# Expert feed-forward in units of 128 rows, four to a group, with the transposed rows copied by VectorE

## The chip, the cores and the metric

The kernel runs on one core of a Trainium2 chip. The metric is the device time of one launch in microseconds. All times below are microseconds of device time unless marked ns. The compute engines are PE (TensorE), DVE (VectorE), ACT (ScalarE) and POOL (GpSimd); SP (SyncE) issues most of the transfers.

## The reference

A batch of 16 sequences of 512 tokens, width 128, passes through four residual blocks: a linear attention, a mixture of experts, a second attention that keeps the 6 strongest rows of each head, and the same mixture again. Cut to the part that the change touches (T = 8192 tokens, E = 16 experts, K = 2 choices, D = H = 128):

```python
x = x + attn_a(layernorm(x))
x = x + ffn(layernorm(x))
x = x + attn_b(layernorm(x))
x = x + ffn(layernorm(x))

def ffn(xf):                                   # xf: [T, D]
    w, idx = top_k(softmax(xf @ router_w), K)  # two experts for each token
    # each expert takes at most `capacity` first choices and as many second
    # choices, in token order; dispatch lists the tokens of each expert
    xe = x_pad[dispatch]
    gate = einsum('ecd,edh->ech', xe, gate_w)
    up = einsum('ecd,edh->ech', xe, up_w)
    out = einsum('ech,ehd->ecd', silu(gate) * up, down_w) * wbuf
    return zeros.at[dispatch].add(out)         # sum of a token's two rows
```

## The kernel before

Each engine has its own program, written out by hand; the order on an engine is the order in the source, and engines meet only in semaphores. The phases are: attention A over 16 batches, the experts of its mixture, attention B, the experts of the second mixture, and a tail that adds the experts' rows into the tokens and stores them.

**Stages.** Each mixture is cut into two halves of 8 batches, so `experts` runs four times. The text calls these stages 0 to 3 (`seg` in the code). Stage 1 follows stage 0 at once, attention B lies between stages 1 and 2, and stage 3 follows stage 2 at once. The tokens of a half are scattered to DRAM (`dispA` or `dispB`) by POOL's indirect transfers, one area for each expert, and the area is read in *units* of `UR` rows that belong to one expert. A table made on chip lists for each unit its first row and its expert. Half a mixture has 48 units of 256 rows, taken in 24 groups of `GU` = 2 units, so that a group is always 512 rows.

**One group, engine by engine.** SP's `load(seg, g)` reads the unit's row numbers from the table into registers (one TENSOR_LOAD, then a check of each value: FUSED_REGOPS and SEQ_ASSERT) and issues one transfer for each unit into `apart` (named `xe`). There are `NX` = 4 such buffers; loads 0 to 3 of a stage are issued ahead, and load g waits for the transposes of group g-4. PE's `turn_x` (L1812) transposes four tiles of rows into one PSUM bank. ACT's `xT` (L846) copies them to `xeT`. PE's `gate_up` (L1823) multiplies with the gate and up weights; ACT's `silu` (L851) and DVE's `hidden` (L1293) form the hidden rows; PE's `down` (L1834) multiplies with the down weights; DVE's `y_copy` (L1301) empties the PSUM bank into `ye`; SP's `store` (L417) writes that to `ybufA` or `ybufB`. PE's order is `turn_x(g+1)`, `gate_up(g)`, `down(g-1)`, then a piece of other work that belongs to group g (`pieces(g)`: routing of the last batches, the end of attention B, the tables of the next stage).

**Weights.** Since the expert of a unit is known only at run time, its 384 weight columns are copied from `f_w` into a ring of group buffers `unit_w`, at an address from a register: by POOL for the first four groups of a stage (L587), by ACT for the others (L858), each copy waiting until the buffer's last `down` is done.

**SP's order in a stage.** For g = 0, 1, ...: `load(g+4)`, then `store(g-2)`, which waits for `y_copy(g-2)`. After its last load of an even stage SP waits until the next stage's table is made and its tokens are sent (`ready`, L400 to L405), then issues load 0 and load 1 of the next stage, the third last store, load 2, the second last store, load 3, and the last store. `y_copy(g)` waits until the store of group g-2 has landed, because there are two `ye` buffers.

**After stages 0 and 2** POOL waits until all stores of the stage have landed (`stored`) and gathers the two expert rows of each token with indirect transfers (`fetch`, L564), eight for a batch. A fetch needs the batch's slot numbers (`slg`), and for batch b these are written by DVE once it has added batch b-2 (`add_all`, which ends in `indices(b + 2)`). In stage 3 DVE adds `EARLY` batches beside the groups, three groups to a batch, beginning at group 5; the others follow behind the stage. `EARLY` is (groups - 4) // 3.

The constants from which the sizes follow:

```python
UT = 2                       # tiles of 128 rows in a unit
UR = UT * P
GU = 2                       # units in a group
NX = 4                       # buffers of rows and of weights
UNITS = -(-(HALFB * SEQ * K // UR + E - 1) // (GU * NX)) * GU * NX
GRP = UNITS // GU            # groups in a stage
```

## Time and profile before

| what | value |
|---|---|
| median of three runs | 1403.18 (1398.74 to 1406.71) |
| the profiled execution | 1396.88 |
| its span, from the first to the last instruction | 1395.1 |
| busy shares of the span | PE 89%, DVE 75%, POOL 60%, ACT 54% |
| chain that ended last | PE 70%, DVE 12%, POOL 7% |

| stretch | from | to | length |
|---|---|---|---|
| attention A, until the first transpose of stage 0 | 0 | 341.6 | 341.6 |
| stage 0 and stage 1 (48 groups) | 341.6 | 503.0 | 161.4 |
| attention B | 503.0 | 1130.1 | 627.1 |
| stage 2 (24 groups) | 1130.1 | 1219.8 | 89.7 |
| stage 3 (24 groups), beside POOL's gathering for the first half | 1219.8 | 1298.7 | 78.9 |
| the rest of the gathering, adding and storing | 1298.7 | 1395.1 | 96.4 |

The share of busy time is a mean over these stretches, and they have different limits. In the expert stages the place to look is the time of one group on each engine and on SP, which is not counted as busy at all; in the tail it is POOL's line of indirect transfers. In a row of the timeline the first number is the start, the second the length, then engine, line, operation, what it writes and reads, and how many were merged; the bracket at the end is the idle time before it and what ended it.

### The profile page before, as it was taken

Reading aid. Unit: us, or ns where it says so; the run is one execution under the profiler, and the core shown is the slowest. Engines: PE = TensorE matmul, PEld = TensorE weight load, DVE = VectorE, ACT = ScalarE, POOL = GpSimd, SP = SyncE. Lnnn points to the kernel's source line nnn. Section 1 sums busy time; section 2 is a strip of 40 time slices with the busy share of each in tenths; the row PEclk is TensorE's granted clock in tenths of the full one; section 3 lists DMA queues with packets and bytes.
Section 4 is the critical chain, followed back from the end, with each engine's and each line's share of the span. In section 5 each row is a group of like instructions: output and inputs, shape, how many; then the busy total and the mean of one; then the engine's idle time right before and its main releaser. Section 6 shows DMA issues by size and latency. Waiting matters only on the chain.

```text
span 1395.1 us, 28372 instructions
## 1 busy us (share of the span) xinstructions
PE 1239.1 (89%) x8534; PEld 787.4 (56%) x8534; DVE 1042.0 (75%) x4462; ACT 756.4 (54%) x1901; POOL 836.4 (60%) x1246
## 2 busy tenths in 40 slices
PE   3999998996999999999999999999999999999100
PEld 1566665565898965454545445545455469888100
DVE  2899999895674458898999989989998856565322
ACT  2444444442665767666676756656676546556000
POOL 3237776777525224356777767766874445367776
PEclk9999999997999998998999989999999899999655
DMA  6845602011556520000100001011000125466522
GB/s 174 259 154 192 197 30 87 28 44 60 171 163 210 166 65 16 14 11 24 32 25 29 32 24 32 29 62 48 29 28 14 44 79 162 150 218 205 150 75 75
DMA packets 119783, 125.80 MB, mean 90 GB/s; under 512 B 15568, under 2 KB 109904, under 8 KB 119632
## 3 DMA queue, kind: packets, MB, share of 16 engines
q1 hardware_dynamic: 103248, 90.42, 20.5%
q0 software_dynamic: 16384, 33.59, 7.9%
q8 instruction: 68, 1.11, 0.3%
q14 instruction: 83, 0.68, 0.2%
HBM read 50.15 MB, written 73.79 MB: 89 GB/s over the span
## 4 chain that ended last, share of the span: by engine, by line
PE 70%; DVE 12%; POOL 7%; issue 4%; DMA 2%; ACT 2%; SPq 0%; POOLq 0%; ACTq 0%; DVEq 0%
PE pair L1897 25%; PE pair L1823 8%; POOL vmyg L564 6%; PE pair L1685 5%; DVE pT L1401 5%; PE bank L1709 4%; PE pair L1834 4%; PE pair L1812 2%; PE bank L1630 2%; PE bank L1624 2%; PE pair L1674 2%; DVE xs L1318 2%; PE bank L1936 1%; PE bank L1916 1%; PE pair L1695 1%
## 5 line engine op out<-in xcount | busy, mean ns | idle before, releaser
L1897 PE MATMUL pair<-kT,apart 32*128 32x512 f32 x2048 | 460.2, 672 | 3.5 <-DVE smax L1401 2.0
L1401 DVE CUSTOM_DVE_ANT_0 pT<-pair,pT 128x256 f32<-128x256 f32 x1024 | 384.2, 416 | 76.1 <-ACT pT L925 70.4
L925 ACT ACTIVATE pT<-pair 128x256 f32<-128x256 f32 x1024 | 327.0, 397 | 196.8 <-PE pair L1897 193.3
L1897 PEld LDWEIGHTS pair<-kT,apart 32*128 32x128 f32 x2048 | 192.8, 192 | 128.1 <-DVE smax L1401 78.7
L564 POOL DMA_INDIRECT vmyg<-ybufA,slg x128 | 123.7, 966 | 110.6 <-DVE smax L1401 67.9
L1823 PE MATMUL pair<-xeT,unit_w 128*128 128x256 f32 x768 | 184.6, 384 | 0.0
L564 POOL DMA_INDIRECT vmyg<-ybufB,slg x128 | 122.8, 959 | 71.3 <-DVE smax L1401 33.6
L509 POOL DMA_INDIRECT dispB<-xnf,sli x128 | 129.3, 1010 | 57.0 <-issue 35.2
L509 POOL DMA_INDIRECT dispA<-xnf,sli x128 | 130.0, 1016 | 50.9 <-issue 30.2
L1128 DVE TENSOR_TENSOR pT<-pair,causal 128x1024 f32<-128x1024 f32 x128 | 151.2, 1213 | 12.1 <-PE pair L1685 11.2
L1293 DVE TENSOR_TENSOR hid<-sg,pair 128x512 f32<-128x512 f32 x96 | 65.7, 685 | 123.3 <-ACT sg L851 123.1
L1823 PEld LDWEIGHTS pair<-xeT,unit_w 128*128 128x128 f32 x768 | 140.5, 193 | 15.5
L1318 DVE SCALAR_TENSOR_TENSOR xs<-vmyg,wts,xs 128x128 f32<-128x128 f32 x248 | 81.1, 379 | 75.4 <-DMA vmyg<-ybufB,slg 55.1
L1834 PE MATMUL pair<-unit_w,hid 128*128 128x128 f32 x768 | 102.1, 276 | 8.6 <-DVE ye L1301 8.4
L1834 PEld LDWEIGHTS pair<-unit_w,hid 128*128 128x128 f32 x768 | 99.9, 192 | 16.2 <-DVE hid L1293 10.6
L858 ACT ACTIVATE unit_w<-f_w 128x384 f32 x160 | 74.9, 515 | 50.1 <-PE pair L1834 47.8
L851 ACT ACTIVATE sg<-pair 128x512 f32<-128x512 f32 x96 | 57.3, 597 | 55.7 <-PE pair L1823 55.3
L1401 DVE DVE_READ_ACCUMULATOR2_ANT smax<- 128x1 f32 x1024 | 82.5, 81 | 0.0
L1685 PE MATMUL pair<-apart,kT 32*128 32x512 f32 x512 | 77.5, 647 | 1.8 <-DVE pT L1128 1.8
L1709 PE MATMUL bank<-pT,vmyg 128*32 128x128 f32 x2048 | 70.9, 280 | 0.0
L1301 DVE COPY ye<-pair 128x512 f32<-128x512 f32 x96 | 65.6, 683 | 6.7 <-DMA ybufA<-ye 4.0
L551 POOL TENSOR_SCALAR lnv<-mv 128x4 f32<-128x4 f32 (+1 forms) x51 | 11.9, 234 | 97.1 <-DVE mv L1024 89.0
(231 smaller groups left out, 1947.6 us busy)
## 6 DMA issues: line engine op xcount, KB each, us to landing
dispB<-zeros SPq DMA_DIRECT2D x16, 1408.0 KB
apart<-dispA SPq DMA_DIRECT2D x96, 128.0 KB
ybufA<-ye SPq DMA_DIRECT2D x48, 256.0 KB
apart<-dispB SPq DMA_DIRECT2D x96, 128.0 KB
ybufB<-ye SPq DMA_DIRECT2D x48, 256.0 KB
dispA<-zeros SPq DMA_DIRECT2D x33, 128.0 KB
xs<-in_x SPq DMA_DIRECT2D x16, 256.0 KB, 3.1
out<-xs SPq DMA_DIRECT2D x15, 256.0 KB, 2.6
```

The lines of the kernel that those rows point to most:

```text
L509: pool.indirect_dma_start(out=area, out_offset=bass.IndirectOffsetOnAxis(ap=sli[h][:, K * j + k:K * j + k + 1], axis=0), in_=xnf[g % NF][: ...
L564: pool.indirect_dma_start(out=yg[h][:, j, :], out_offset=None, in_=ybuf[second(g)], in_offset=bass.IndirectOffsetOnAxis(ap=slg[h][:, j:j + ...
L858: last = act.activation(unit_w[g % NX][:, u, :], f_w[:, bass.ds(ex[u], 1), :].rearrange("p a n -> p (a n)"), ACT.Copy)
L925: act.activation(rel[n % RING][:, q, :], pair[n % RING][:, q, HALF:SEQ], ACT.Relu).then_inc(s["relu_done"], 1)
L1128: dve.tensor_tensor(pTd[n % NG][:, :, :], pair[1 + n % 2][:, :, :].rearrange("p q (j t) -> p (q j) t", j=GH), causal[:, :].unsqueeze(1).to ...
L1318: last = dve.scalar_tensor_tensor(out=xb, in0=yg[h][:, K * j + k, :], scalar=wts[:, bass.ds((b * TB + j) * K + k, 1)], in1=xb, op0=ALU.mul ...
L1401: dve.tensor_tensor_reduce(out=rel[n % RING][:, q, :], in0=pair[n % RING][:, q, 0:HALF], in1=rel[n % RING][:, q, :], scale=1.0, scalar=LOW ...
L1685: pe.matmul(bank[4 + g][:, :].rearrange("p (j t) -> p j t", j=GH), kTs[h][at, c * P:(c + 1) * P], apart[h][at, :, c * P:(c + 1) * P], star ...
L1709: last = pe.matmul(bank[1][at:at + QG, c * P:(c + 1) * P], vm[:, c, j * P + at:j * P + at + QG], pT[c % 2 * NG + g][:, j, :], start=(c == ...
L1823: last = pe.matmul(bank[3 + 2 * h + k][:, u * UR:(u + 1) * UR], unit_w[r][:, u, k * D:(k + 1) * D], xeT[h][:, UT * u:UT * (u + 1), :].rear ...
L1834: last = pe.matmul(bank[7][:, j * D:(j + 1) * D], hid[h][:, j, :], unit_w[r][:, j // UT, 2 * D:3 * D], start=True, stop=True)
L1897: pe.matmul(pair[n % RING][:, q, :], apart[h][at, j, t * P:(t + 1) * P], kTs[h][at, HALF:], start=True, stop=True).then_inc(s["bsc_done"], 1)
```

## The change

A unit becomes 128 rows and a group four units, so a group is still 512 rows. A half has 80 units instead of 48, hence 20 groups instead of 24. Each group now has four row loads instead of two (64 KB each instead of 128 KB), eight matmul calls of 128 columns in `gate_up` instead of four of 256, and four weight copies instead of two; the `unit_w` ring shrinks from four group buffers to three, so that a copy for group g waits for `down(g-3)`. The transposed rows are copied by DVE and no longer by ACT. The pieces of stage 2 from group 13 on move one or two groups forward, `EARLY` falls from 6 to 5, and the areas of `dispA` and `dispB` are cleared in pieces of half the length.

```diff
-UT = 2
+UT = 1
-GU = 2
+GU = 4
+NW = 3
-        unit_w = [sb(f"unit_w{r}", [P, GU, 3 * D]) for r in range(NX)]
+        unit_w = [sb(f"unit_w{r}", [P, GU, 3 * D]) for r in range(NW)]
...
@@ gpsimd, copies
-                if at >= NX:
-                    pool.wait_ge(s["y_done"], at - NX + 1)
+                if at >= NW:
+                    pool.wait_ge(s["y_done"], at - NW + 1)
...
-            send_beside(2 * B - 1, B - 1, 1, 17)
-            for g in range(NX):
+            send_beside(2 * B - 1, B - 1, 1, 15)
+            for g in range(NW):
                 copies(3, g)
...
@@ scalar, experts
-                def xT(g):
-                    act.wait_ge(s["xe_tp"], g + 1 + base)
-                    act.activation(xeT[g % 2][:, :, :].rearrange("p j d -> p (j d)"), bank[2][:, :],
-                                   ACT.Copy).then_inc(s["xeT_ready"], 1)
...
-                    act.wait_ge(s["y_done"], base + g - NX + 1)
+                    act.wait_ge(s["y_done"], base + g - NW + 1)
...
-                xT(0)
                 for g in range(G):
-                    if g + 1 < G:
-                        xT(g + 1)
                     silu(g)
-                    if 2 <= g < G - 2:
+                    if NW - 2 <= g < G - 2:
                         copies(g + 2, weights_of(mybir.EngineType.Activation, seg, g + 2, 1))
...
@@ vector, experts
+                def xT(g):
+                    dve.wait_ge(s["xe_tp"], g + 1 + base)
+                    dve.tensor_copy(xeT[g % 2][:, :, :].rearrange("p j d -> p (j d)"), bank[2][:, :]).then_inc(s["xeT_ready"], 1)
...
+                xT(0)
                 for g in range(G):
+                    if g + 1 < G:
+                        xT(g + 1)
                     hidden(g)
                     if g:
                         y_copy(g - 1)
...
@@ vector, pieces of stage 2
-                if g == 16:
+                if g == 15:
+                    route_ranks(b + B, bank[0])
...
@@ tensor, gate_up and down
-                    h, r = g % 2, g % NX
+                    h, r = g % 2, (base + g) % NW
```

On SP's queue, in the loop of a stage, a load and the store behind it read so before (`tableA` holds rows and experts of the units, `apart` the loaded rows; ISA are the checks and addresses in registers):

```order
L385 TENSOR_LOAD tableA [waits xe_tp]
L385 ISA x4
L388 ISA
L388 DMA apart<-dispA 128x256
L388 ISA
L388 DMA apart<-dispA 128x256
L417 DMA ybufA<-ye 128x2x256 [waits y_ready]
```

and now:

```order
L386 TENSOR_LOAD tableA [waits xe_tp]
L386 ISA x8
L389 ISA
L389 DMA apart<-dispA 128x128
L389 ISA
L389 DMA apart<-dispA 128x128
L389 ISA
L389 DMA apart<-dispA 128x128
L389 ISA
L389 DMA apart<-dispA 128x128
L418 DMA ybufA<-ye 128x4x128 [waits y_ready]
```

Between two stores there are now four transfers with an address each and eight checks, where there were two and four.

On ACT, one group in the middle of a stage read so before:

```order
L846 ACTIVATE xeT<-pair 128x512 [waits xe_tp]
L851 ACTIVATE sg<-pair 128x512 [waits gu_done]
L326 TENSOR_LOAD tableA
L326 ISA x4
L858 ISA [waits y_done]
L858 ACTIVATE unit_w<-f_w 128x384
L858 ISA
L858 ACTIVATE unit_w<-f_w 128x384
```

and now:

```order
L847 ACTIVATE sg<-pair 128x512 [waits gu_done]
L327 TENSOR_LOAD tableA
L327 ISA x8
L854 ISA [waits y_done]
L854 ACTIVATE unit_w<-f_w 128x384
L854 ISA
L854 ACTIVATE unit_w<-f_w 128x384
L854 ISA
L854 ACTIVATE unit_w<-f_w 128x384
L854 ISA
L854 ACTIVATE unit_w<-f_w 128x384
```

The copy of the transposed rows is gone from here, and two weight copies with their addresses and four checks have come in.

## Rows read from the trace of the kernel before

**Rows 1.** Stretches: length, then busy time of PE, PEld, DVE, ACT, POOL; granted clock; stage 1

```profile
425.00:503.00 78.00, 76.01 (x489) 69.47 (x487) 37.51 (x80) 48.79 (x95) 24.38 (x31) 1.00 0.55 172
```

**Rows 2.** Timeline of PE: one group of stage 0 and the next one's transposes

```profile
407.52 0.60 PE L1812 MATMUL pair<-ident,apart 128*128 128x128 f32 x4
407.96 1.89 PE L1823 MATMUL pair<-xeT,unit_w 128*128 128x256 f32 x8
409.69 1.05 PE L1834 MATMUL pair<-unit_w,hid 128*128 128x128 f32 x8
410.58 0.60 PE L1812 MATMUL pair<-ident,apart 128*128 128x128 f32 x4
```

**Rows 3.** Timeline of SP: two loads in a burst; two loads with a store between

```profile
1132.00 0.33 SPq L388 DMA_DIRECT2D apart<-dispA  x1
...
1134.08 0.85 SPq L388 DMA_DIRECT2D apart<-dispA  x2
...
422.41 0.85 SPq L388 DMA_DIRECT2D apart<-dispB  x2
423.31 0.43 SPq L417 DMA_DIRECT2D ybufA<-ye  x1
424.95 0.33 SPq L388 DMA_DIRECT2D apart<-dispB  x1
```

**Rows 4.** SP's register work by line: count, least/median/most ns of one, when

```profile
L385 SPq FUSED_REGOPS  x192: 152/152/159, 308.9 to 1279.1; - x192
L385 SPq TENSOR_LOAD <-tableB x48: 462/472/920, 418.5 to 1278.4; - x48
...
L312 SPq TENSOR_LOAD <-tails x32: 264/273/476, 222.9 to 945.4; - x32
```

**Rows 5.** The same of the clearing transfers, 1408 and 128 pieces in one

```profile
L313 SPq DMA_DIRECT2D dispA<-zeros x32: 332/333/908, 223.9 to 946.1; - x32
L378 SPq DMA_DIRECT2D dispB<-zeros x16: 533/534/4932, 49.3 to 166.1; - x16
```

**Rows 6.** Timeline of PE: first transposes of stage 0 and 2, last products of stage 1 and 2

```profile
341.62 1.12 PE L1812 MATMUL pair<-ident,apart 128*128 128x128 f32 x4
...
501.90 1.13 PE L1834 MATMUL pair<-unit_w,hid 128*128 128x128 f32 x8 [1.21 <-DVE ye L1301]
...
1130.13 0.66 PE L1812 MATMUL pair<-ident,apart 128*128 128x128 f32 x4 [1.54 <-DVE smax L1401]
...
1218.66 1.13 PE L1834 MATMUL pair<-unit_w,hid 128*128 128x128 f32 x8 [1.21 <-DVE ye L1301]
```

**Rows 7.** Timeline of DVE: the last ranks of the routing, and stage 2's last copy

```profile
1197.48 0.29 DVE L1105 TENSOR_REDUCE rank<-rkoh 128x8 f32<-128x128 f32 x1
...
1220.34 0.69 DVE L1301 COPY ye<-pair 128x512 f32<-128x512 f32 x1 [1.83 <-DMA ybufA<-ye]
```

**Rows 8.** Timeline of SP at the end of stage 2, and of POOL's gathers

```profile
1214.86 0.36 SPq L388 DMA_DIRECT2D apart<-dispB  x1
...
1217.87 0.43 SPq L417 DMA_DIRECT2D ybufA<-ye  x1
...
1223.20 0.43 SPq L417 DMA_DIRECT2D ybufA<-ye  x1
...
1227.58 1.99 POOL L564 DMA_INDIRECT vmyg<-ybufA,slg  x1 [5.64 <-DMA ybufA<-ye]
...
1309.03 0.94 POOL L564 DMA_INDIRECT vmyg<-ybufB,slg  x1 [0.30 <-issue]
```

**Rows 9.** Timeline of POOL and ACT at the end of attention A

```profile
318.53 0.96 POOL L587 COPY unit_w<-f_w 128x384 f32 x2 [0.31 <-issue]
...
333.46 1.65 ACT L784 ACTIVATE xnf<-xs,nmr,rstd 128x128 f32<-128x128 f32 x4 [12.23 <-POOL nmr L556]
```

**Rows 10.** Stretch of stage 2: length, PE's busy time, granted clock, DMA share, GB/s

```profile
1192.00:1196.00 4.00, 2.86 (x23) 1.00 0.19 66
```

**Rows 11.** Timeline of ACT: the weight copies of one group in stage 0

```profile
405.14 0.94 ACT L858 ACTIVATE unit_w<-f_w 128x384 f32 x2 [0.77 <-PE pair L1834]
```

More of the change, by code:

```diff
@@ L192, in build @@
         apart = [sb(f"apart{h}", [P, GH, SEQ]) for h in range(2)]
-        whose = sb("whose", [P, NT * K, E])
+        whose = sb("whose", [P, HALFB * TB * K, E])
         xe = [[apart[h][:, r, :].rearrange("p (j d) -> p j d", d=D) for r in range(NX)] for h in range(2)]
@@ L581, in copies @@
                     pool.wait_ge(s["w_in2"], 16 * 11)
-                if at >= NX:
-                    pool.wait_ge(s["y_done"], at - NX + 1)
+                if at >= NW:
+                    pool.wait_ge(s["y_done"], at - NW + 1)
                 ex = weights_of(mybir.EngineType.Pool, seg, g, 1)
                 for u in range(GU):
-                    last = pool.tensor_copy(unit_w[g % NX][:, u, :], f_w[:, bass.ds(ex[u], 1), :].rearrange("p a n -> p (a n)"))
+                    last = pool.tensor_copy(unit_w[at % NW][:, u, :], f_w[:, bass.ds(ex[u], 1), :].rearrange("p a n -> p (a n)"))
                 last.then_inc(s["unit_w_ready"], 1)
@@ L653, in stored @@
                     pool.wait_ge(s[f"y_out{h}"], AHEAD + 16 * (seg + 1) * GRP // 2)
-            for g in range(NX):
+            for g in range(NW):
                 copies(1, g)
@@ L685, in body @@
                 if not next:
-                    for g in range(NX):
+                    for g in range(NW):
                         copies(2, g)
@@ L751, in _ @@
             places(B - 1, 2 * B - 1, 1)
-            send_beside(2 * B - 1, B - 1, 1, 17)
-            for g in range(NX):
+            send_beside(2 * B - 1, B - 1, 1, 15)
+            for g in range(NW):
                 copies(3, g)
@@ L854, in copies @@
                 def copies(g, ex):
-                    act.wait_ge(s["y_done"], base + g - NX + 1)
+                    act.wait_ge(s["y_done"], base + g - NW + 1)
                     for u in range(GU):
-                        last = act.activation(unit_w[g % NX][:, u, :], f_w[:, bass.ds(ex[u], 1), :].rearrange("p a n -> p (a n)"),
+                        last = act.activation(unit_w[(base + g) % NW][:, u, :], f_w[:, bass.ds(ex[u], 1), :].rearrange("p a n -> p (a n)"),
                                               ACT.Copy)
                     last.then_inc(s["unit_w_act"], 1)
-                xT(0)
                 for g in range(G):
-                    if g + 1 < G:
-                        xT(g + 1)
                     silu(g)
-                    if 2 <= g < G - 2:
+                    if NW - 2 <= g < G - 2:
                         copies(g + 2, weights_of(mybir.EngineType.Activation, seg, g + 2, 1))
@@ L1558, in pieces @@
                     table_slots(2, (g - 11,))
+                if g == 13:
+                    route_max(b + B, bank[0])
                 if g == 14:
-                    route_max(b + B, bank[0])
+                    route_top(b + B)
                 if g == 15:
-                    route_top(b + B)
+                    route_ranks(b + B, bank[0])
                 if g == 16:
-                    route_ranks(b + B, bank[0])
+                    table_counts(3, bank[0])
                 if g == 17:
-                    table_counts(3, bank[0])
-                if g == 18:
                     table_starts(3)
                     table_rows(3)
+                if g == 18:
+                    table_copy(3, bank[0])
                 if g == 19:
-                    table_copy(3, bank[0])
-                if g == 20:
                     indices(0, 0)
@@ L1828, in down @@
                 def down(g):
-                    h, r = g % 2, g % NX
+                    h, r = g % 2, (base + g) % NW
                     pe.wait_ge(s["hid_done"], g + 1 + base)
@@ L2072, in pieces @@
                     scatter_context(b)
-                if g == 13:
+                if g == 12:
                     pe.wait_ge(s["rk_done"], 2 * B)
                     turn(b + B, "ffn", xnf[(b + B) % NF])
-                if g == 14:
+                if g == 13:
                     logits(b + B, bank[0])
-                if g == 16:
+                if g == 15:
                     pe.wait_ge(s["lsub_done"], 2 * B)
                     ranks(b + B, bank[0])
-                if g == 17:
+                if g == 16:
                     pe.wait_ge(s["rk_done"], 2 * B + 1)
                     counts(3, bank[0])
-                if g == 19:
+                if g == 18:
                     table_rows(3, bank[0])
```

7 lines of the change are left out of this document (3 added, 4 removed).

## The prediction

> **What bounds the kernel now.** I read the stretches first, for what is busy where, then the timeline of one group in a stage, and then the queue that no busy share shows, SP's. In the expert stages the bound is PE: in stage 1 it is busy for 76.0 of 78 us at the full granted clock of 1.00, and ACT, DVE and POOL are at 24 to 49 [rows 1]. Within a group PE runs without a gap: the transposes start at 407.52, gate and up at 407.96, down at 409.69, the next transposes at 410.58 [rows 2]. So a group costs 0.44 + 1.73 + 0.89 = 3.06 us of PE.
>
> SP is close behind. In a burst, where nothing holds it back, the first transfer of one load starts at 1132.00 and that of the next at 1134.08: 2.08 us for a load of two units. With a store in between it is 422.41 to 424.95, 2.54 us, so a store costs 0.46 [rows 3]. PE needs 3.06 us a group and hides that today, with half a microsecond to spare.
>
> In the tail POOL sets the pace: its gathers run from 1227.58, after stage 2's stores, without a break of note to the end, and those for the second half begin at 1309.03 [rows 8]. Stage 3 lies under the first half of them. The end of the kernel therefore hangs on three things: when stage 1 ends, when stage 2 ends and its stores land, and how fast POOL may gather.
>
> **The change part by part.**
>
> PE's work in a group stays: the same columns pass through gate and up, in pieces of 128 with a weight load each, and `down` already has that shape at 0.89 us for half as many [rows 2], so gate and up take 2 x 0.89 = 1.78 instead of 1.73. Four groups fewer in each stage are worth 4 x 3.06 = 12.2 us of PE a stage, if PE stays the bound.
>
> SP's work in a group grows, by its register work and its transfers. Two transfers in one load take 0.85 us, one 0.33, so each further one costs 0.52 [rows 3]. Each further value costs its check: the operation alone is 0.15 [rows 4], and the 1.23 us from the end of one load's last transfer to the next load's first [rows 3], less 0.47 for the register load, leave 0.38 for each of the two values with all that stands around them. I take 0.29, since an address and its gaps belong to that too. That makes 2.08 + 2 x (0.52 + 0.29) = 3.70 us for a load of four units. The register load itself is the unknown: no row has one of four values. With one value it takes 0.27 us, with two 0.47 [rows 4]. Either the second value cost 0.20 and the next two will too (4.10 us for the load), or it stays at 0.47 (3.70). I take 4.10, the straight line through the two rows, and keep 3.70. The store has 512 pieces instead of 256; the clearing transfers give 0.20 us for 1280 more pieces [rows 5], hence 0.04, and I take 0.50 (bound 0.46). So SP's cycle becomes 4.6 us a group (4.2 at the lower bound) and passes PE's 3.06. SP becomes the bound of every expert stage, and what is gained in the number of groups is lost in the length of one.
>
> No row shows a register load of four values, and the Trainium skill has two rules on it that disagree. The Trainium skill, page "DMA: Bandwidth & Descriptors", section "Latency and other measured facts", gives tensor_load a floor of about 600 ns; by that four values would cost little more than two, and the time would be that of rival 2 below. The trace is below that floor with 273 ns for one value [rows 4]. The Trainium skill, page "Runtime: NRT & Kernel Launch", section "Instruction fetch mechanics", gives about 200 ns a register for loads of another kind; by that the time would be the forecast's, and the step from 273 to 472 ns agrees.
>
> *POOL at the end of attention A.* POOL copies the first weights there, and right behind them it is on the path: ACT starts the last norm as soon as POOL has its scale [rows 9]. Four groups of two copies at 0.96 + 0.31 = 1.27 us were 5.1; three groups of four, with 4 x 0.48 us of copies and some register work, are 5.8 to 8. I add 2 (bounds 0 and 3).
>
> *Stages 0 and 1.* The first transposes end at 342.7 [rows 6]. From there SP has 36 loads (16 of stage 0, four being there already, and 20 of stage 1) and 33 stores up to stage 1's last load: 36 x 4.1 + 33 x 0.5 = 164.1. Two waits come on top. `y_copy(g)` needs the landing of the store of g-2; DVE does wait for that today at the end of stage 2, 2.5 us after the store's issue [rows 7, 8], and the later store takes over 3.5 until POOL goes on [rows 8], so I take 3.0. When SP sets the pace, the store of group 13 follows the last load, so `y_copy(15)` ends 0.5 + 3.0 + 0.7 = 4.2 us after that load. Then come `down(16)` 0.9 and two more groups as today, 8.0 (from the last transposes to the last product: 0.44 + 2 x 1.73 + 2 x 0.89 and 2.3 for the last wait and product, as in [rows 6]): the stage ends 13.1 us after its last load. And SP itself waits at the seam for `y_copy(15)` and `(16)`, 4.4 us. Stage 1 ends at 342.7 + 2 + 164.1 + 4.4 + 13.1 = 526.3, against 503.0 today: **+23.3** (+5 at the lower bound). Pieces and stalls that cost PE about 14 us in these two stages today are covered by SP's pace and cost nothing more; if that cover fails they come on top.
>
> *Stage 2.* Sixteen loads and 13 stores from 1130.8 on [rows 6]: 65.6 + 6.5 + 13.1 = 85.2, an end at 1216.0 against 1219.8: **-3.8** (-10.7). The gain comes from the 16 us of routing pieces that PE carries today and that SP's pace now covers.
>
> *The seam of stages 2 and 3.* Call stage 2's end E. Today POOL begins to gather at E + 7.8 [rows 6, 8]. SP issues the next stage's loads ahead of the last stores, and it may begin them when the last tokens are sent. From the last ranks at 1197.77 to the first such transfer at 1214.86 it is 17.1 us [rows 7, 8], 1.5 of them register work: 15.6. The ranks move to group 15, behind `y_copy(14)`, which waits for store 12, so they come about when SP ends its last load, E - 13.1. From there 15.6, four loads 16.4 and two stores 1.0 lead to the last store at E + 19.9, and 4.4 later (1223.20 to 1227.58 [rows 8]) POOL gathers, at E + 24.3.
>
> *Stage 3 and the gathers.* Batch 2 can be gathered when DVE has added batch 0, in group 6, behind `y_copy(5)` and so behind the landing of store 3: six loads and three stores after the seam, E + 20.4 + 24.6 + 1.5, then 3.0 + 0.7 + 2.1 give E + 52.3, while POOL is free at E + 44.7. From there each batch takes DVE three groups, 13.8 us, where POOL needs 10.2: batch 5 at E + 93.7. From then on POOL sets the pace again, and the second half begins three batches later, at E + 124.3, against E + 89.2 today [rows 8]: **+35.1** (+27). Behind it nothing changes.
>
> DVE's third copy and ACT's two more copies cost nothing as long as SP's cycle is 4.6. DVE's three copies are 2.05 us a group, at the 0.69 of [rows 7]. ACT's silu 0.6 and four copies, twice the 0.94 of [rows 11], are 2.5, with register work ahead of them that overlaps the silu. At PE's 3.06 both would be near the edge.
>
> Sum: 23.3 - 3.8 + 35.1 = +54.6 on a span of 1395.1. The profiled execution took 1396.88, 6.3 less than the median of the runs, 1403.2. On the median the forecast is 1457; at the lower bounds +21, 1424.
>
> **The rivals.**
> 1. *SP stays hidden, and PE gets its gain.* It needs an SP cycle of at most 3.06 us. Stages 0 and 1 then give back 24.5, stage 2 12.2, POOL takes 2: 1369, faster. Against it: two more transfers alone bring the 2.54 of [rows 3] to 3.58. For it: only that no row shows four transfers in a line. 0.07.
> 2. *The register load does not grow.* The same mechanism at 4.2 us a group: 1424, still slower. 0.2.
> 3. *The waits at the seams are hidden after all, and stage 2 gains more.* If the seams cost nothing and DVE's adds keep up with POOL, rival 2 loses another 20: about 1404, no change. 0.04.
> 4. *TensorE's clock falls.* PE would idle a third of each group. At the lower of its two levels, 1.2 GHz, a group takes 6.1 us and passes SP's 4.6: 1.5 us for each of 60 groups, up to 90 on top. Against it: a stretch with PE busy for 2.86 of 4.0 us keeps its 1.00 [rows 10]. 0.05, beyond the range.
>
> **How the numbers follow.** The forecast has 0.64: 1440 to 1475 with the unabsorbed pieces above and shorter landings below. With rival 2 (1415 to 1440) that is 0.84, and the range is 1415 to 1475. About 7 us, 0.5%, is what a measurement of this kernel can tell from no change. Faster by more 0.07, within 0.04, slower by more 0.89.
>
> **What would show it.** Right: SP's transfers of one group 4.6 us apart in stages 0 and 1 with no wait before the loads; PE with idle time in each group ahead of transposes or `down`, ended by a transfer or `ye`; a register load of four values of 0.8 to 0.9 us; POOL's first gather some 24 us after stage 2's last product, and gaps between its batches 2 to 6 that end with `slg`. Wrong: groups at 3.1 us; SP waiting for PE's transposes in every group; a granted clock below 1.00 inside the stages; or PE waiting for the copy of the transposed rows by DVE.

## The result, and the profile after

The changed kernel takes 1434.05 us (median of four runs, 1429.04 to 1437.79) against 1401.33 for the kernel before on the same chip: 1.0227 times as long, interval 1.0200 to 1.0253. That is slower, and within the forecast's range of 1415 to 1475, but 23 us below its 1457. The profiled execution has a span of 1432.3, 37.2 more than the 1395.1 of before; the forecast had +54.6.

Where the 37.2 us come from, by the same marks in both timelines (E is the end of stage 2's last product):

| part | before | after | measured | forecast |
|---|---|---|---|---|
| attention A, to stage 0's first transpose | 341.6 | 347.0 | +5.4 | +2 |
| stages 0 and 1 | 161.4 | 169.8 | +8.4 | +21.3 |
| attention B | 627.1 | 629.6 | +2.5 | 0 |
| stage 2, to E | 89.7 | 88.1 | -1.6 | -3.8 |
| from E to the first gather of the second half's rows | 89.2 | 111.4 | +22.2 | +35.1 |
| from there to the end | 86.1 | 86.4 | +0.3 | 0 |

PE no longer fills the stages. In the two stretches of stages 0 and 1 (length, busy time of PE, PEld, DVE, ACT, POOL, then granted clock, DMA share and GB/s) it is idle for 11.5 of 83 and 15.5 of 87 us. Before it was 3.4 of 83.4 us in stage 0, and 2 of 78 in stage 1 [rows 1]:

```profile
347.00:430.00 83.00, 71.50 (x600) 69.29 (x597) 58.28 (x161) 47.87 (x98) 36.86 (x60) 0.95 0.45 134
430.00:517.00 87.00, 71.49 (x572) 67.69 (x570) 45.13 (x93) 45.34 (x95) 25.39 (x34) 0.96 0.46 134
```

Within a group the work is what it was in [rows 2], 0.44 to gate and up and 1.79 for gate and up when nothing waits (the rows of e1 below). What is new are the brackets: PE waits for `ye` and for `xeT`, and the second transposes start 4.59 us after the first. PE's timeline in stage 1:

```profile
478.29 0.60 PE L1811 MATMUL pair<-ident,apart 128*128 128x128 f32 x4
478.73 1.95 PE L1822 MATMUL pair<-xeT,unit_w 128*128 128x128 f32 x16
481.23 1.13 PE L1833 MATMUL pair<-unit_w,hid 128*128 128x128 f32 x8 [0.56 <-DVE ye L1297]
482.88 0.63 PE L1811 MATMUL pair<-ident,apart 128*128 128x128 f32 x4 [0.52 <-DVE xeT L1290]
```

Both waits lead back to SP. `y_copy` on DVE waits for the landing of the store of two groups before, and the copy of `xeT` stands behind it, and behind a piece of DVE's sums, on the same queue. DVE's timeline of that group:

```profile
480.39 0.69 DVE L1297 COPY ye<-pair 128x512 f32<-128x512 f32 x1 [1.58 <-DMA ybufB<-ye]
...
482.05 0.68 DVE L1290 COPY xeT<-pair 128x512 f32<-128x512 f32 x1
```

SP's timeline at the end of stage 0 answers [rows 3]. From one load to the next it is 400.81 - 396.90 = 3.91 us, and 404.74 - 400.81 = 3.93, without a break. Over the whole of stage 1, from the register load of its first group (422.40) to that of its last (499.04), the mean is 4.03 us a group. So SP's cycle did pass PE's 3.06; the forecast had 4.6:

```profile
396.90 1.88 SPq L389 DMA_DIRECT2D apart<-dispA  x4
398.83 0.43 SPq L418 DMA_DIRECT2D ybufA<-ye  x1
400.81 1.88 SPq L389 DMA_DIRECT2D apart<-dispA  x4
...
404.74 1.88 SPq L389 DMA_DIRECT2D apart<-dispA  x4
```

SP's register work (count, least, median and most ns of one) tells why it is less. The checks are as in [rows 4], 0.15 each, but a register load of four values takes 0.30 us, where two values took 0.47 and the forecast had 0.86:

```profile
L386 SPq FUSED_REGOPS  x320: 147/147/159, 313.1 to 1312.3; - x160
L386 SPq TENSOR_LOAD <-tableA x40: 295/303/549, 312.7 to 1210.9; - x40
L386 SPq TENSOR_LOAD <-tableB x40: 295/301/311, 422.4 to 1311.2; - x40
```

The ends of the stages, and the seam behind stage 2, on PE (answering [rows 6]):

```profile
347.03 1.12 PE L1811 MATMUL pair<-ident,apart 128*128 128x128 f32 x4
...
515.68 1.13 PE L1833 MATMUL pair<-unit_w,hid 128*128 128x128 f32 x8 [1.21 <-DVE ye L1297]
...
1146.40 0.66 PE L1811 MATMUL pair<-ident,apart 128*128 128x128 f32 x4 [1.54 <-DVE smax L1400]
...
1233.41 1.13 PE L1833 MATMUL pair<-unit_w,hid 128*128 128x128 f32 x8 [1.21 <-DVE ye L1297]
1239.20 1.12 PE L1811 MATMUL pair<-ident,apart 128*128 128x128 f32 x4 [4.66 <-DMA apart<-dispB]
```

The seam on SP and POOL (answering [rows 8]). SP waits for the last sent tokens; its first transfer of stage 3 goes out at E + 1.2, and eight go out ahead of the first of stage 2's last three stores; the last of these is issued at 1249.31, E + 14.8. POOL gathers from 1252.58, E + 18.0 (before E + 7.8), and then waits for `slg` ahead of four batches, 13.2 us in all. The second half's rows begin at 1345.93, E + 111.4:

```profile
1235.77 5.69 SPq L389 DMA_DIRECT2D apart<-dispB  x8
1241.51 0.43 SPq L418 DMA_DIRECT2D ybufA<-ye  x1
...
1249.31 0.43 SPq L418 DMA_DIRECT2D ybufA<-ye  x1
...
1252.58 1.01 POOL L565 DMA_INDIRECT vmyg<-ybufA,slg  x1 [14.29 <-DMA ybufA<-ye]
...
1279.15 0.94 POOL L565 DMA_INDIRECT vmyg<-ybufA,slg  x1 [6.58 <-DVE slg L1312]
...
1291.11 0.95 POOL L565 DMA_INDIRECT vmyg<-ybufA,slg  x1 [2.25 <-DVE slg L1312]
...
1345.93 0.94 POOL L565 DMA_INDIRECT vmyg<-ybufB,slg  x1 [0.30 <-issue]
```

The view of waits sums up what PE waits for in the stages (us in all, times, longest). The second row is a wait that the forecast had put at nothing; 10.6 us of it, 11 times, lie in stages 0 and 1:

```profile
PE pair L1833 <- DVE ye L1297: 23.6, 20, 2.8
PE pair L1811 <- DVE xeT L1290: 22.9, 22, 5.1
```

### The profile page after: what moved, and what is told of

Its sections match the earlier page's. It is cut to its first block, busy times and chain, and to the rows that moved or that the text cites. A ratio compares the mean times of both kernels' runs of the same rounds, so it can differ in the third digit from the quotient of the medians.

```text
span 1432.3 us, 29988 instructions
## 1 busy us (share of the span) xinstructions
PE 1220.9 (85%) x8854; PEld 777.8 (54%) x8854; DVE 1076.1 (75%) x4510; ACT 742.4 (52%) x1901; POOL 841.7 (59%) x1262
## 4 chain that ended last, share of the span: by engine, by line
PE 62%; DVE 11%; issue 6%; SPq 6%; POOL 5%; DMA 3%; ACT 3%; ACTq 1%; POOLq 0%; DVEq 0%
PE pair L1896 25%; PE pair L1684 5%; PE pair L1822 4%; PE bank L1708 4%; DVE pT L1400 4%; POOL vmyg L565 4%; SPq L389 3%; PE bank L1629 2%; SPq L386 2%; PE bank L1623 2%; PE pair L1673 2%; PE pair L1811 2%; DMA ybufB<-ye 1%; DVE xs L1317 1%; PE bank L1915 1%
## 5 line engine op out<-in xcount | busy, mean ns | idle before, releaser
L1822 PE MATMUL pair<-xeT,unit_w 128*128 128x128 f32 x1280 | 165.8, 286 | 0.3 <-DVE xeT L1290 0.3
L1822 PEld LDWEIGHTS pair<-xeT,unit_w 128*128 128x128 f32 x1280 | 159.5, 203 | 0.5 <-DVE xeT L1290 0.5
L854 ACT ACTIVATE unit_w<-f_w 128x384 f32 x272 | 119.8, 511 | 66.8 <-PE pair L1833 63.0
L1833 PE MATMUL pair<-unit_w,hid 128*128 128x128 f32 x640 | 87.3, 280 | 23.6 <-DVE ye L1297 23.6
L1285 DVE TENSOR_TENSOR hid<-sg,pair 128x512 f32<-128x512 f32 x80 | 54.7, 684 | 61.2 <-ACT sg L847 60.8
L1297 DVE COPY ye<-pair 128x512 f32<-128x512 f32 x80 | 54.9, 687 | 59.0 <-DMA ybufB<-ye 42.3
L847 ACT ACTIVATE sg<-pair 128x512 f32<-128x512 f32 x80 | 47.6, 595 | 88.7 <-PE pair L1822 88.1
L1833 PEld LDWEIGHTS pair<-unit_w,hid 128*128 128x128 f32 x640 | 78.6, 193 | 27.1 <-issue 18.8
L1811 PE MATMUL pair<-ident,apart 128*128 128x128 f32 x320 | 53.4, 293 | 30.6 <-DVE xeT L1290 22.9
L552 POOL TENSOR_SCALAR lnv<-mv 128x4 f32<-128x4 f32 (+1 forms) x51 | 12.4, 243 | 112.6 <-DVE mv L1016 105.9
```

What stands on the lines that cost most here:

```text
L854: last = act.activation(unit_w[(base + g) % NW][:, u, :], f_w[:, bass.ds(ex[u], 1), :].rearrange("p a n -> p (a n)"), ACT.Copy)
L1811: last = pe.transpose(bank[2][:, j * P:(j + 1) * P], xe[seg % 2][r][:, j, :], ident[:, :])
L1822: last = pe.matmul(bank[3 + 2 * h + k][:, u * UR:(u + 1) * UR], unit_w[r][:, u, k * D:(k + 1) * D], xeT[h][:, UT * u:UT * (u + 1), :].rear ...
L1833: last = pe.matmul(bank[7][:, j * D:(j + 1) * D], hid[h][:, j, :], unit_w[r][:, j // UT, 2 * D:3 * D], start=True, stop=True)
```

## The experiments

For all profiled executions, one of each kernel, the same marks, in us. "Gathers" are the first gather and the first gather of the second half's rows, after E; the clock is the granted clock of attention B, where PE's work is the same in all of them:

| kernel | median | span | stages 0, 1 | attention B (clock) | stage 2 | gathers |
|---|---|---|---|---|---|---|
| before | 1401.33 | 1395.1 | 161.4 | 627.1 (0.96) | 89.7 | 7.8, 89.2 |
| after | 1434.05 | 1432.3 | 169.8 | 629.6 (0.95) | 88.1 | 18.0, 111.4 |
| e1_no_checks | 1401.47 | 1397.9 | 150.8 | 633.5 (0.94) | 88.2 | 13.5, 96.6 |
| e2_units_alone | 1430.07 | 1428.1 | 166.0 | 633.5 (0.94) | 86.0 | 18.1, 110.3 |
| e3_copy_alone | 1419.63 | 1417.9 | 171.9 | 634.1 (0.94) | 93.5 | 6.5, 88.5 |
| e4_stores_first | 1439.89 | 1445.5 | 176.6 | 637.1 (0.93) | 87.7 | 5.3, 111.8 |
| e5_reads_four | 1421.47 | 1419.8 | 172.8 | 633.4 (0.94) | 89.5 | 10.0, 94.4 |
| e6_units_no_checks | 1393.08 | 1391.4 | 144.4 | 636.6 (0.94) | 85.5 | 14.7, 95.6 |
| e7_before_no_checks | 1408.00 | 1408.0 | 158.8 | 644.2 (0.92) | 90.0 | 4.7, 85.7 |
| e8_adds_in_two | 1430.47 | 1432.3 | 169.9 | 637.1 (0.93) | 87.7 | 17.9, 107.0 |
| e9_stores_before_wait | 1397.15 | 1400.0 | 144.3 | 645.9 (0.92) | 83.4 | 5.0, 95.0 |
| e10_sums_from_three | 1393.77 | 1392.2 | 144.3 | 647.7 (0.92) | 83.4 | 5.1, 89.0 |
| e11_reads_aligned | 1403.86 | 1402.1 | 163.8 | 629.9 (0.95) | 89.8 | 7.5, 88.0 |

From the first gather of the second half's rows to the end it is 85.7 to 86.4 us in all of them. The medians of e5 and e11 are single runs. The kernel before, run beside each group of experiments, had medians of 1401.49 (e1 to e4), 1400.06 (e5 to e8) and 1400.48 (e9 to e11), and the ratios below are to these.

### e1_no_checks: is it SP's queue?

```diff
@@ sync, load (kernel after)
-                    table[seg % 2][0:1, g * GU:g * GU + GU], engines=[mybir.EngineType.SP], min_val=0, max_val=DUMMY)[1]
+                    table[seg % 2][0:1, g * GU:g * GU + GU], engines=[mybir.EngineType.SP], min_val=0, max_val=DUMMY,
+                    skip_runtime_bounds_check_because="the table is made on chip from unit counts and lies within the area")[1]
```

> The changed kernel, with the range checks of the row numbers left out on SP alone; every transfer, wait and sum stays. Theory (SP's queue sets the pace of a group): SP's cycle falls from 3.91 us by four checks of about 0.27 to about 2.8, below PE's 3.1. The transposes of neighbouring groups then start 3.1 to 3.3 apart, stages 0 and 1 shrink from 169.8 to 145 to 152 us, stage 2 from 88 to about 80, and the kernel lands at 1380 to 1400. Rival 1 (the third copy on DVE, ahead of PE's gate and up, sets the pace): nothing changes, 1430 to 1438. Rival 2 (four small transfers land too slowly): the groups stay near 3.9 although SP is done early, 1425 to 1438.

Measured: 1401.47, 0.9993 of before (interval 0.9967 to 1.0019), so 33 us of the change's loss are gone when nothing but SP's queue gets shorter. SP's loads now follow each other in 2.9 us where its transfers don't stall, and in the middle of stage 1 PE runs as in [rows 2], 474.12 - 471.00 = 3.12 us from transposes to transposes:

```profile
471.00 0.60 PE L1812 MATMUL pair<-ident,apart 128*128 128x128 f32 x4
471.44 1.95 PE L1823 MATMUL pair<-xeT,unit_w 128*128 128x128 f32 x16
473.23 1.06 PE L1834 MATMUL pair<-unit_w,hid 128*128 128x128 f32 x8
474.12 0.60 PE L1812 MATMUL pair<-ident,apart 128*128 128x128 f32 x4
```

The bound that the prediction named is shown by that, but not for every stage. From the transposes of group 4 to those of group 19, fifteen groups, it takes (us):

| stage | before | after | e1 |
|---|---|---|---|
| 0 | 49.8 | 56.8 | 54.8 |
| 1 | 48.0 | 64.6 | 50.1 |
| 2 | 55.3 | 64.0 | 64.0 |
| 3 | 47.4 | 62.6 | 48.8 |

In stages 1 and 3 nearly all of the loss is SP's. In stage 0 it is 1.9 of 7 us, and in stage 2, where the expectation was about 80 us, SP's checks cost nothing: 88.2 us, as in after, and the groups follow each other as they did there. The first and the last transposes of stage 2 are 78.40 us apart in after and 78.41 in e1:

```profile
1146.40 0.66 PE L1811 MATMUL pair<-ident,apart 128*128 128x128 f32 x4 [1.54 <-DVE smax L1400]
...
1224.80 0.60 PE L1811 MATMUL pair<-ident,apart 128*128 128x128 f32 x4
```

```profile
1127.24 0.65 PE L1812 MATMUL pair<-ident,apart 128*128 128x128 f32 x4 [1.54 <-DVE smax L1401]
...
1205.65 0.60 PE L1812 MATMUL pair<-ident,apart 128*128 128x128 f32 x4
```

The time itself missed the expected range by 1.5 us: stages 0 and 1 give 10.6 us back against before, of a possible 24.5, and stage 2 no more than 1.5.

### e2_units_alone and e3_copy_alone: the two parts of the change apart

e2 is the kernel after with the copy of xT on ScalarE again; e3 is the kernel before with that copy on VectorE (its definition moves with these calls):

```diff
@@ e3, scalar
-                xT(0)
                 for g in range(G):
-                    if g + 1 < G:
-                        xT(g + 1)
                     silu(g)
...
@@ e3, vector
+                xT(0)
                 for g in range(G):
+                    if g + 1 < G:
+                        xT(g + 1)
                     hidden(g)
```

> Units of 128 rows, four to a group, as in the changed kernel, with the copy of the transposed rows back on ACT. Theory: SP has the same 3.9 us a group, so 1428 to 1442. Rival (the copy on DVE is what costs the time): back to within 10 us of the kernel before, 1392 to 1411.

> The kernel before, in units of 256 rows, with nothing but the copy of the transposed rows moved from ACT to DVE. Theory: PE keeps 3.06 us a group outside the pieces, DVE's 2.05 us of copies fit in; 1398 to 1412, no change to 0.8% slower (DVE's pieces of over 1 us now hold up the next transposes). Rival (the copy costs the time): 1420 to 1440.

Measured: e2 1430.07, 1.0199 (1.0157 to 1.0241); the smaller units make the loss, and VectorE's copy adds nothing to it that these runs can tell (after: 1.0200 to 1.0253). e3 1419.63, 1.0113 (1.0074 to 1.0151), above what was expected and at the lower edge of its rival: where PE is the bound, the copy on VectorE costs by itself. PE's timeline in stage 0 of e3 shows how. DVE carries the routing of the last batches beside the groups, the copy stands behind it on that queue, and PE waits 2.00 us. The gate and up products behind the wait then take 3.33 us instead of 1.89:

```profile
355.80 0.91 PE L1811 MATMUL pair<-ident,apart 128*128 128x128 f32 x4 [2.00 <-DVE xeT L1290]
356.51 3.33 PE L1822 MATMUL pair<-xeT,unit_w 128*128 128x256 f32 x8
...
361.23 1.89 PE L1822 MATMUL pair<-xeT,unit_w 128*128 128x256 f32 x8
```

In the stretches of e3 around it the granted clock (the first of the last three numbers) is 1.00, then 0.66 where the wait ends, and 1.00 again: between the two levels, 1.2 and 2.4 GHz, in the middle stretch. Here the products behind a wait of 2.0 us take 1.4 us longer:

```profile
352.00:355.00 3.00, 1.80 (x13) 1.47 (x11) 2.96 (x20) 0.60 (x1) 0.00 (x0) 1.00 0.34 87
355.00:360.00 5.00, 4.20 (x15) 3.61 (x16) 4.20 (x18) 0.12 (x1) 1.14 (x3) 0.66 0.25 77
360.00:364.00 4.00, 4.00 (x34) 3.78 (x33) 2.10 (x4) 2.02 (x4) 2.72 (x5) 1.00 0.36 117
```

Of e3's 22.8 us on the span, 10.5 lie in stages 0 and 1, 3.8 in stage 2, 2.3 ahead of stage 0, and 7.0 in attention B with its lower clock. So about 14 us lie where the copy is.

### e4_stores_first: the order at the seams

```diff
@@ sync, experts (kernel after)
-                if seg % 2 == 0:
-                    ready(seg + 1)
-                    load(seg + 1, 0)
-                    load(seg + 1, 1)
                 store(GRP - 3)
-                if seg % 2 == 0:
-                    load(seg + 1, 2)
                 store(GRP - 2)
-                if seg % 2 == 0:
-                    load(seg + 1, 3)
                 store(GRP - 1)
+                if seg % 2 == 0:
+                    begin(seg + 1)
```

> The changed kernel, with the last three stores of stage 0 and stage 2 issued before the loads of the next stage instead of among them. Theory (the loads of the next stage delay the stores and so POOL's gathers, but the gathers of batches 2 to 6 then wait for DVE's adds in stage 3): POOL's first gather comes 6 to 8 us after stage 2's last product instead of 18, and yet the end moves by 0 to 5 us, 1429 to 1436. Rival (the seam itself costs the 10 us): 1422 to 1426.

Measured: 1439.89, 1.0259 (1.0220 to 1.0298), above the expected range and about 6 us over after, though the two intervals overlap; certainly not the 1422 to 1426 of the rival. The first gather does come sooner, E + 5.3 instead of E + 18.0, but POOL then waits 18.94 us for `slg` ahead of the third batch, since DVE's sums hang on the groups of stage 3, and these begin no sooner; the second half's rows begin at E + 111.8, as in after (111.4). At the seam of stages 0 and 1 the loads now wait for the last store, and its first transposes come 16.1 us after the last ones of stage 0, instead of 9.2.

### e5_reads_four and e11_reads_aligned: the price of a register load

```diff
@@ e5: the kernel before
-  table[seg % 2][0:1, g * GU:g * GU + GU]
+  table[seg % 2][0:1, g * GU:g * GU + 2 * GU]
@@ e11: the kernel before
-  table[seg % 2][0:1, g * GU:g * GU + GU]
+  table[seg % 2][0:1, g // 2 * 4:g // 2 * 4 + 4]
...
-  disp[seg % 2][bass.ds(rows[u], UR), :]
+  disp[seg % 2][bass.ds(rows[g % 2 * 2 + u], UR), :]
```

> The kernel before, in which SP reads four values of the table for each load and uses the first two. It measures the term of my sum that was mis-sized by itself. Theory (the price of a register load hangs on how its values are counted, not on the units): TENSOR_LOAD on SP falls from .47 to about .30, as in the kernel after; two more range tests add .57, so SP's cycle becomes 2.54 + .57 - .17 = 2.94 us, still under TensorE's 3.06, and the time stays within 0.5% of before. Rival (the load got shorter for another reason in the kernel after, such as the wait before it): it stays at .47 or grows, SP's cycle passes 3.1 to 3.5 and the expert stages get longer, 1410 to 1425.

> The kernel before, in which SP reads for each load the four values that begin at a multiple of four values in the table, and uses two of them. In e5 a load of four values took .30 us at even groups (its first value at a multiple of 16 bytes) and 1.23 to 1.56, or .87, at odd ones (8 bytes past one). Theory (where the four values begin decides the price): all loads take .30, SP's cycle is 2.54 + .57 - .17 = 2.94 us, under TensorE's 3.06, and the time is that of before within 0.5%. Rival (something else that alternates, such as which buffer is stored beside it): every other load is still over .8, and the time is about 1420.

Measured for e5: 1421.47, and neither theory holds as written. Two register loads of SP one after the other, of 0.30 and of 1.31 us (answers of the view by line for two short stretches):

```profile
L385 SPq TENSOR_LOAD <-tableB x1: 301/301/301, 441.0 to 441.0; - x1
...
L385 SPq TENSOR_LOAD <-tableB x1: 1313/1313/1313, 443.9 to 443.9; - x1
```

The short and the long ones alternate with the groups. At even groups the four values begin at a multiple of 16 bytes, counted from the table's start, at odd ones 8 bytes past it. In e11 they always begin at a multiple, and all loads are short:

```profile
L385 SPq TENSOR_LOAD <-tableA x48: 295/302/583, 311.3 to 1208.8; - x48
L385 SPq TENSOR_LOAD <-tableB x48: 295/300/309, 422.0 to 1289.5; - x48
```

e11's time, 1403.86, is that of before (1400.48 in that comparison) within 0.3%. So what decides for four values is where they begin: from a multiple of 16 bytes they take 0.30, from 8 bytes past one 0.86 to 1.56. Two take 0.47 at even and odd groups alike. e5, a single run, is a second sign of SP's part, on the kernel before: with 0.57 us of checks and the long load its cycle in odd groups is about 3.9 us, its mean about 3.4, over PE's 3.06, and stages 0 and 1 take 172.8.

### e6_units_no_checks and e7_before_no_checks: a faster version and its control

Both leave the range checks out on SP, ScalarE and GpSimd; e6 is the kernel of e2 (small units, xT on ScalarE), e7 the kernel before.

```diff
@@ weights_of (load as in e1)
-                table[seg % 2][0:1, at:at + count * GU], engines=[eng], min_val=0, max_val=E - 1)[1]
+                table[seg % 2][0:1, at:at + count * GU], engines=[eng], min_val=0, max_val=E - 1,
+                skip_runtime_bounds_check_because="the table holds numbers of experts")[1]
```

> The kernel after, with the copy of xT on ScalarE again and without the range tests of the table's values on SP, ScalarE and GpSimd. SP theory with VectorE's copy as a second cost: both costs that the change brought are gone, and what is left is fewer padded rows; the groups of stages 0, 1 and 3 come every 3.1 to 3.4 us, stages 0 and 1 take 140 to 152 (151 with the copy on VectorE), and the time is 1380 to 1398. Rival (ScalarE is next: xT .58, four weight copies 1.76, silu .60 and its gaps are 3.1 to 3.7 us of each group): groups of 3.7, 1400 to 1412.

> The kernel before without the range tests of the table's values on SP, ScalarE and GpSimd: the control for the runs in which SP's tests are left out. Theory (before, TensorE sets the pace at 3.06 us a group and SP's 2.54 hides behind it): same within 0.5%, 1394 to 1402. Rival (the tests cost wherever they stand, at the seams above all): 1380 to 1392, and the gain of leaving them out says less on SP's cycle.

Measured: e6 1393.08, 0.9953 of before (0.9925 to 0.9981), within the expected range: with SP's queue short and the copy off VectorE, small units are a little faster than the kernel before. Stages 0 and 1 take 144.4 us, 17.0 less than before, and most groups come every 3.1 us, not the 3.7 of the rival. The gain of stages 2 and 3 is not there: stage 2 is 4.2 shorter, but the second half's gathers begin 6.4 later after E, and attention B, which is the same code, is 9.5 longer at its lower clock.

e7 is 1408.00, 1.0051 (1.0030 to 1.0073): not the "same" of the theory, nor the gain of the rival. Its stages 0 and 1 are 2.6 us shorter and its gathers 3.5 sooner, so the checks do cost a little even under PE; but attention B takes 644.2 us. As the control it says that without SP as the bound the checks are worth a few us in the stages, so e1's 33 are not a gain that any kernel would have. One stretch of attention B, of e7 and then of before, shows the granted clock at 0.80 and at 0.98 while PE is busy for 98.96 and 97.06 of 100 us:

```profile
900.00:1000.00 100.00, 98.96 (x434) 46.14 (x431) 80.51 (x446) 57.45 (x171) 63.60 (x88) 0.80 0.14 44
```

```profile
900.00:1000.00 100.00, 97.06 (x490) 47.83 (x490) 92.00 (x502) 66.57 (x199) 72.17 (x97) 0.98 0.15 48
```

### e8_adds_in_two: DVE's sums and POOL's gathers

```diff
@@ vector, pieces of stage 3 (kernel after)
-            EARLY = (GRP - 4) // 3
+            EARLY = 7
-                if g >= 5 and (g - 5) % 3 < 2 and (g - 5) // 3 < EARLY:
-                    add_all((g - 5) // 3, ((g - 5) % 3,))
+                if g >= 5 and (g - 5) // 2 < EARLY:
+                    add_all((g - 5) // 2, ((g - 5) % 2,))
```

> The kernel after, with VectorE's sums of the second half put at every second group of stage 3 and not at two of every three. It measures the last step of my prediction by itself. Theory (the gathers of the second half wait 13 us in all for the row numbers that stand behind those sums): the waits of POOL for slg after the first one, 2.25 + 2.61 + 1.73 us, go, the gathers of the other half's rows begin 5 to 8 us sooner after the end of stage 2 (111 before, 103 to 106 now), and the time is 1425 to 1430. Rival (the end is set by the last stores of stage 3, or the sums hold TensorE's groups back by what they give): 1432 to 1436.

Measured: the waits for `slg` behind the first are gone as expected, and the second half's rows begin at E + 107.0 instead of E + 111.4. That is 4.4 us, not 5 to 8, because the gathers now catch up with the last stores of stage 3 and wait 2.38 us for them. The time, 1430.47 (1.0203, interval 1.0165 to 1.0241), is half a microsecond over the expected range, at the low end of after's runs, and can't be told from after: the profiled execution lost 7.5 us in attention B.

### e9_stores_before_wait and e10_sums_from_three: the seam in the faster version

```diff
@@ sync, experts (kernel of e6)
+                if seg == 2:
+                    store(GRP - 3)
+                    store(GRP - 2)
+                    store(GRP - 1)
+                    begin(3)
+                    return
@@ vector, pieces of stage 3, in e10 alone
-            EARLY = (GRP - 4) // 3
+            EARLY = 6
-                if g >= 5 and (g - 5) % 3 < 2 and (g - 5) // 3 < EARLY:
-                    add_all((g - 5) // 3, ((g - 5) % 3,))
+                if g >= 3 and (g - 3) % 3 < 2 and (g - 3) // 3 < EARLY:
+                    add_all((g - 3) // 3, ((g - 3) % 3,))
```

> The kernel of e6, in which SP issues the last three stores of stage 2 ahead of its wait for stage 3's tables and sent tokens, and then stage 3's first loads (at the seam of stages 0 and 1 nothing is changed). In e6 SP stands in that wait until 1211 and the last store goes out at 1221, after eight more loads; TensorE's last product of stage 2 ends at 1209.8. Theory (the first gather waits for the last store alone, and the sums of VectorE, which are tied to stage 3's groups, then hold the third batch of gathers): the first gather comes 5 to 10 us sooner after that product (14.8 in e6), POOL then waits 4 to 8 us for slg at the third batch, where it waited 0.3, and the second half's gathers begin 2 to 5 us sooner; 1388 to 1393. Rival (the seam is worth what the prediction gave it, with nothing given back): 8 to 10 us, 1383 to 1386.

> As e9, with VectorE's sums of the second half begun at group 3 of stage 3 and not at group 5 (six batches in place of five lie beside the groups). Theory: POOL's wait for slg at the third batch goes, so the whole of the seam counts: the second half's gathers begin 8 to 10 us sooner after stage 2's last product than in e6, and the time is 1382 to 1388. Rival (the sums hold TensorE's groups, or the last stores of stage 3 come too late for the second half's gathers): like e9 or worse.

Measured: the steps are those of the theory, their sizes are not. In e9 POOL's first gather comes at E + 5.0 instead of 14.7, and 9.07 us go back at the third batch, where 4 to 8 were expected; the second half's rows begin at E + 95.0, where e6 has 95.6, no more than 0.6 sooner and not 2 to 5. The timeline of POOL in e9:

```profile
1224.08 1.02 POOL L573 DMA_INDIRECT vmyg<-ybufA,slg  x1 [0.16 <-issue]
...
1253.81 0.94 POOL L573 DMA_INDIRECT vmyg<-ybufA,slg  x1 [9.07 <-DVE slg L1321]
```

In e10 the sums come two groups sooner, the wait is 1.65, and the second half's rows begin at E + 89.0, 6.6 sooner than in e6, where 8 to 10 were expected. Its timeline of POOL:

```profile
1245.72 0.95 POOL L573 DMA_INDIRECT vmyg<-ybufA,slg  x1 [1.65 <-DVE slg L1321]
...
1306.13 0.95 POOL L573 DMA_INDIRECT vmyg<-ybufB,slg  x1 [0.30 <-issue]
```

The times missed the expected ranges too: e9 1397.15, 0.9971 (0.9941 to 1.0001), e10 1393.77, 0.9927 (0.9893 to 0.9960). What the seam gives in the profile, attention B takes back (645.9 and 647.7 us at a clock of 0.92). e10 is faster than the kernel before; it can't be told from e6.

## Why the prediction was right, and which terms were off

**The mechanism was right, but it does not hold in every stage.** SP's queue became the bound of stages 1 and 3: 3.9 to 4.1 us a group, PE idle, and with SP's checks left out 14.6 and 13.8 us of fifteen groups are gone (e1). It delayed the seam and the gathers behind stage 2 by the chain of the forecast: stores behind the next stage's loads, the first gather later, DVE's sums tied to the groups. "SP becomes the bound of every expert stage" was wrong for stage 2, and for most of stage 0.

**The register load was mis-sized**, and with it SP's cycle. The straight line through one and two values gave 0.86 us; it is 0.30, and even the lower bound, 0.47, was too high. Neither of the two rules that the prediction weighed gives 0.30 for four values. The other terms of the load stood: the forecast's 3.70 with 0.30 in the place of 0.47 is 3.53, and measured are 3.91 - 0.43 = 3.48, with 0.43 for the store. So the cycle is 3.91 instead of 4.6. Put into the forecast's own formula (36 loads, 33 stores, 4.4 and 13.1) this alone takes 36 x 0.62 + 33 x 0.07 = 24.6 us off stages 0 and 1. The Trainium skill, page "SBUF — State Buffer", section "Specifications (TRN2)", says that the memory is organised in lines of 16 bytes, with a penalty for each cross into another; e5 and e11 agree with that as far as the start of the four values decides (0.30 against 0.86 to 1.56 us), though that section speaks of bandwidth and not of register loads. That two values, which never pass the end of such a line here, take 0.47 is not explained by it.

**The cover was mis-sized the other way.** By the formula with the measured cycle stages 0 and 1 would have been 21.3 - 24.6 = 3.3 us shorter than before; they are 8.4 longer, so 11.7 us came back. The prediction had said that PE's pieces and stalls, about 14 us, are covered by SP's pace, and that they come on top where that cover fails. It ran SP's loads as one line from stage 0's first transposes on. But SP enters stages 0 and 2 with four loads done. In stage 0 the register load of group 4 is 15.8 us ahead of that group's transposes, that of group 19 9.0; in stage 2 it is 13.7 and 13.9; in stage 1, where SP is the bound, it is 6.0 to 9.6. While SP has the longer lead, its slower cycle covers nothing, which fits the small gain of e1 in stage 0 and none in stage 2. To that came what the prediction put at nothing, DVE's third copy. Where PE is the bound that copy alone costs 10.5 us in stages 0 and 1 (e3); in the changed kernel 3.8 (169.8 against e2's 166.0). Part of PE's 10.6 us of waits for `xeT` is SP's doing, as the rows of stage 1 show: in that stage they are 4.9 us, and 1.3 in e1. The two errors, of opposite sign, leave the term at +8.4 where 21.3 stood. How the rest of the 11.7 us divides was not measured.

**Stage 2 came near by luck.** The forecast had -3.8, the measured change is -1.6. With the measured cycle the same formula gives -3.8 - (16 x 0.62 + 13 x 0.07) = -14.6, and e1 shows that SP does not set the pace there. PE is busy for 77.4 of the 88.1 us, with its pieces in 20 groups instead of 24.

**The seam was right in kind and too long.** The whole term was +35.1 and measured +22.2. Four loads and two stores took SP 13.5 us, from 1235.77 to 1249.31, instead of 17.4, and the last store needed 3.3 instead of 4.4 to let POOL go: E + 18.0, not 24.3. DVE's three groups a batch were 12.0 to 12.4 us instead of 13.8: E + 111.4, not 124.3. Both go with the shorter cycle. e8 and e9 confirm the chain behind it: loosen the sums, and 4.4 us come back; loosen the stores alone, and nothing does.

**Left out: TensorE's clock outside the stages.** In attention A the clock at 240 to 252 was 0.58, before 0.86; 12 us at 0.28 less make 3.4 us, an estimate. In e1, with 0.86 there, stage 0 begins at 342.9 instead of 347.0. Attention B is 2.5 longer, so together 5.9 of the 37.2. POOL's first copies, put at 2, cost about 1: all twelve took 5.61 us. Rival 4 in the form written, PE's idle time halving the clock through the stages, did not come: the mean was 0.95 and 0.96 in stages 0 and 1 (0.97 and 1.00 before), though single products were as slow as in e3, 3.33 us behind a wait of 2.79 for `ye` in stage 1.

**Signs and rivals.** Of the signs of being right, the register load of 0.8 to 0.9 us and the cycle of 4.6 did not come; PE's waits for `ye` and POOL's gaps for `slg` did. Of the signs of being wrong two came: a clock below 1.00 in the stages, and PE waiting for DVE's copy. Rival 2, that the register load does not grow, was the nearest: its condition held, with more to spare than it asked for, and the result lies within the 1415 to 1440 that it was given, 10 us above its 1424. The forecast's own case, 1440 to 1475, did not hold the result; the range did, because it took rival 2 in. Rival 3 did not come: the seam was not hidden. Rival 1 needs an SP cycle under 3.06; with it (e6) the gain is 0.5% and not 2.4%: stages 0 and 1 give 17.0 us, but the second half's gathers, which set the tail, start no sooner after E, and attention B is longer.

## What to carry to other kernels

Cutting work into smaller units multiplies what is paid for each unit on the issuing queue (address, checks, transfer); compare that queue's cycle with the engine's per group before counting what the engine gains. A loop that two engines pace almost equally does not hide the small waits of either, so the cover between them must be costed like any other term. A queue that begins some buffers ahead sets the pace only when that lead is used up, so ask for each stage by itself which queue does; leaving one cost out of one queue, as in e1, shows it. When one wait is shortened, follow the chain to what is tied to other work: here the stores gave 10 us to the gathers, and the sums took 9 of them back until they were moved too.

## What the runs showed of the hardware that was not expected

- A register load of four values that begin at a multiple of 16 bytes takes 0.30 us, less than one of two values (0.47); from 8 bytes past a multiple it takes 0.86 to 1.56 (e5, e11).
- A value's range check on SP costs more than its 0.15 us: without them SP's cycle falls from 3.91 to about 2.9, 0.25 for each of four values (after, e1).
- A wait of 2.00 us on PE is followed by products at 3.33 us in place of 1.89, with a granted clock of 0.66 in that stretch (e3).
- Attention B, the same code in all kernels, takes 627 to 648 us, in step with its granted clock, 0.96 to 0.92. It does not follow the length of the expert stages: e7, with 158.8 us for stages 0 and 1, has 644.2, and e1, with 150.8, has 633.5. What sets that clock stays open. Against the profiled execution of before it took 6 to 21 us of the spans of e1, e6, e7, e9 and e10, and e7 is slower than before though its stages 0 and 1 are shorter.
